# A fused two-block transformer with experts: the exponent's bias moved from VectorE to ScalarE, and the hand-kept order of the work planned anew

## The chip, the cores and the metric

One NeuronCore of a Trainium2 chip runs the whole program. The metric is the device time of one execution in microseconds. Three executions of the kernel before took 3205.08, 3207.56 and 3210.16 us; the median is 3207.56 us.

## The reference, cut to what matters

The input is 8 batches of 512 tokens of 256 numbers. Block L0 normalises, does self-attention and then cross-attention whose operands are rounded to 8 bits, and a gated feed-forward; block L1 does a causal self-attention, a cross-attention and a layer of 8 experts of which each token takes two. The change touches only the two quantised attentions of L0 (stage 0 and stage 1 of each batch):

```python
def _fq(x, delta, zp, n_bits):
    xi = _round_ste(x / delta) + zp
    xq = jnp.clip(xi, 0.0, 2.0 ** n_bits - 1.0)
    return (xq - zp) * delta

sim = jnp.einsum('bhid,bhjd->bhij', _fq(q, dq, 128.0, 8), _fq(k, dk, 128.0, 8)) * SCALE
attn = jax.nn.softmax(sim, axis=-1)
out = jnp.einsum('bhij,bhjd->bhid', _fq(attn, dw, 0.0, 8), _fq(v, dv, 128.0, 8))
```

There are 16 heads of 16 numbers. The softmax is made as exp(scale * s - scale * max), and the product scale * (-max) is the bias that this case is about.

## The kernel before, in words

The program has a transformer part (`transformer`, up to about 2640 us of the span) and behind it an experts part (`experts`). The transformer part is a list of about sixty kinds of steps for every batch B, stage s (0 and 1 quantised attention, 2 feed-forward, 3 and 4 exact attention, 5 and 6 last norm and routing) and number n. `program_steps` says what each step must wait for. `program_order` plays all steps through with `TIMES` (ns that a step takes of its engine, ns until its result is there), `HOPS` (ns from an engine's result to another engine) and `OWN_RESULT` (pairs of kinds where an engine waits for its own result). At every point it picks, among the steps that can start within `AHEAD` ns of the first one, the one with the highest rank: its distance to the end of the program plus an offset from the table `URGENT`. The resulting list `ORDER` is fixed when the program is built, and each engine issues its own kinds (table `ON`) in exactly this order. So an engine whose next step is not ready holds all its later steps back. Where the planner leaves TensorE a gap of `WARM_GAP` (400 ns) or more it puts in matmuls `W` whose result nobody reads (L1678).

A quantised attention stage has 32 units (`UNITS`) of two heads and 128 rows each; over 8 batches and 2 stages that makes 512 units. One unit u runs through this chain:

- `S` (TensorE, L1780): two matmuls put the scores 128x1024 into two PSUM banks. The banks come free when `E` of unit u-2 has read them.
- `M` (VectorE, L1493): `tensor_reduce` with max and negation gives `nmax`, 128x2.
- `nb` (VectorE, L1496): `tensor_scalar` multiplies `nmax` by the stage's scale, a column of `sc`, and gives `nbias`, 128x2. It waits for the engine's own `M`.
- `E` (ScalarE, L1645), twice, one per head: the exponential of 128x512 with `nbias` as bias and `sc` as scale, and the row sums. The first waits for `nb`.
- `R` and `RS` (VectorE, L1499 and L1502): the reciprocal of the row sums, and its product with the quantisation step, `rstep`.
- `Q` (GpSimd, L1263), twice: multiplies by `rstep` and rounds to integers in float16. It waits for `RS`.
- `T` (TensorE, L1788): 8 transposes. `ev` (VectorE, L1509): brings them to SBUF. `AV` (TensorE, L1800): the product with the values.

The exact attentions have their own chain: `A` (TensorE, L1811), `am` (VectorE, L1517, 1024 row maxima), `ms` (GpSimd), `MT` (TensorE), `mt` (ScalarE, L1653), `B` (TensorE, L1833), `E2` (ScalarE, L1664 and L1666), `AV2` (TensorE, L1850). The planner lays a quantised stage of one batch beside an exact stage or the feed-forward of another. ScalarE also empties the PSUM banks of the projections (L1560, L1590, L1606, L1613, L1614, L1620, L1627).

The two lines on VectorE that make the bias:

```python
if kind == "nb":
    after(dve, "M", B, s, n)
    nc.vector.tensor_scalar(nbias[:, n % 2, :], nmax[:, n % 2, :], sc[:, s:s + 1], None, ALU.mult).then_inc(SIG["nb"], 1)
```

Of the kernel before, what the change touches and what calls it, by code (L numbers as in the profile page):

```python
# [6 lines left out]
ALU = mybir.AluOpType  # L7
ACT = mybir.ActivationFunctionType
# [70 lines left out]
def place_taken(B):  # L79
# [29 lines left out]
ON = {"PE": "rT rL rP W S T AV A MT B AV2 xT cT k q v y g w z",  # L109
# [6 lines left out]
ROUTING_OPENS = ("A", 6, 3, 0)  # L116
AHEAD = 84
TIMES = {
# [6 lines left out]
    "own": (3600, 3600), "pkk": (1300, 5500), "pkq": (500, 4500), "psk": (500, 2700), "psq": (1300, 4500), "qi": (330, 417),  # L125
# [18 lines left out]
HOPS = {("PE", "DVE"): 38, ("PE", "ACT"): 38, ("DVE", "PE"): 70, ("ACT", "PE"): 80, ("POOL", "PE"): 56, ("DVE", "ACT"): 36, ("DVE", "POOL"): 83, ("ACT", "DVE"): 60, ("ACT", "POOL"): 80, ("POOL", "DVE"): 60, ("POOL", "ACT"): 90, ("PE", "POOL"): 40}  # L144
OWN_RESULT = {("M", "nb"), ("R", "RS"), ("ki", "ki"), ("qi", "qi"), ("vi", "vi"), ("spk", "spk"), ("spq", "spq"), ("xn", "gb"), ("xn", "bi"), ("rs", "xn"), ("dy", "st"), ("rl", "rl")}
URGENT = {
# [28 lines left out]
    ("pkk", 3): (18222,), ("pkk", 4): (-279907,), ("pkq", 3): (-102687,), ("pkq", 4): (-210459,), ("psk", 3): (70270,),  # L175
    ("psk", 4): (-17390,), ("psq", 3): (180111,), ("psq", 4): (157149,), ("q", 0): (-11596,), ("q", 1): (-58692,),
# [4 lines left out]
    ("spk", 3): (57020,), ("spk", 4): (-35279,), ("spq", 3): (58304,), ("spq", 4): (35133,), ("st", 0): (1581,),  # L181
# [6 lines left out]

# [607 lines left out]
def transformer(nc, scratch, by_row, x, ctx, w, mid, rows_in, kept, s_sc, s_zeroed, s_eb, s_block, s_expert):  # L796
# [41 lines left out]
    with ExitStack() as es:  # L838
# [24 lines left out]
        sc = sb("sc", [P, 4], F32)  # L863
# [7 lines left out]
        xn = sb("xn", [P, NT, D], F32)  # L871
        xT = sb("xT", [P, KT, N], F32)
# [425 lines left out]
        def _(dve):  # L1298
# [15 lines left out]
            for at, e in enumerate(ORDER):  # L1314
# [175 lines left out]
                if kind == "M":  # L1490
                    after(dve, "S", B, s, n)
                    a = BANKS[("S", B, s, n)][0]
                    nc.vector.tensor_reduce(nmax[:, n % 2, :], ps[:, a:a + 2, :], AX.X, ALU.max, negate=True).then_inc(SIG["M"], 1)  # L1493
                if kind == "nb":
                    after(dve, "M", B, s, n)
                    nc.vector.tensor_scalar(nbias[:, n % 2, :], nmax[:, n % 2, :], sc[:, s:s + 1], None, ALU.mult).then_inc(SIG["nb"], 1)  # L1496
                if kind == "R":
# [35 lines left out]
        def _(act):  # L1533
# [8 lines left out]
            for at, e in enumerate(ORDER):  # L1542
# [90 lines left out]
                if kind == "do":  # L1633
                    m = n
                    after(act, "AV", B, s, 2 * NT * m + 2 * NT - 1)
                    stage = before(Q_STAGES, B, s)
                    if stage and m == 0:
                        after(act, "y", *stage, NT - 1)
                    nc.scalar.activation(oTq[:, m, :], OUTQ, ACT.Identity, scale=sc[:, 2 + s:3 + s]).then_inc(SIG["do"], 1)
                if kind == "E":  # L1640
                    u, h = n // 2, n % 2
                    if h == 0:
                        after(act, "nb", B, s, u)
                    after_ordinal(act, "Q", NO[e] - 4)
                    nc.scalar.activation(probs[:, u % 2, h, :], ps[:, BANKS[("S", B, s, u)][h], :], ACT.Exp,  # L1645
                                         bias=nbias[:, u % 2, h:h + 1], scale=sc[:, s:s + 1],
                                         accum_out=rsum[:, u % 2, h:h + 1]).then_inc(SIG["E"], 1)
# [855 lines left out]
```

## Time and profile before

| | us |
|---|---|
| median of three executions | 3207.56 |
| the profiled execution, its own time | 3203.77 |
| span from its first to its last instruction | 3202.0 |
| TensorE busy | 2905.9 (91% of the span) |
| VectorE busy | 2257.2 (70%) |
| ScalarE busy | 1960.0 (61%) |
| GpSimd busy | 1497.5 (47%) |
| mean granted TensorE clock | 0.967 |

The span is 1.8 us shorter than the execution's own time. The busy times count an instruction from its start to its end, so two instructions of one engine that overlap are both counted within a group's sum. The share of the span is a mean over parts with different limits: the transformer part and the experts part are to be read apart, which the view by stretches allows.

### The profile page before, as it was taken

To read this page: it belongs to the slowest core of one execution; us is meant where nothing else is said; L and a number is where in the kernel's file an instruction comes from. 1 tells how busy PE (TensorE), PEld (TensorE's weight loads), DVE (VectorE), ACT (ScalarE), POOL (GpSimd) and SP (SyncE) were. 2 spreads that over 40 slices of the span, in tenths; PEclk is the share of its full clock that TensorE was granted. 3 is DMA by queue.
4 is the path that set the end of the run, shared out by engine and by line. 5 is a ranking of instruction groups with operands and counts; after the bars stand their busy time and mean duration, and the time that the engine had idled before them with its cause. 6 is when DMAs were issued, how large, how long until landed. Compare 5 with 4: busy or idle time off the path is not lost. (4 is left out here: it accounts for less than half of the span.)

```text
span 3202.0 us, 57992 instructions
## 1 busy us (share of the span) xinstructions
PE 2905.9 (91%) x19128; PEld 1688.7 (53%) x19128; DVE 2257.2 (70%) x5109; ACT 1960.0 (61%) x4167; POOL 1497.5 (47%) x2258
## 2 busy tenths in 40 slices
PE   5999989999999999899989999998889899999991
PEld 2445443544354445444543544354444459999991
DVE  3797797989798879978897989798856643111115
ACT  3676676765767676767676765766536354444442
POOL 4654482567266626644682667265714622111115
PEclk9999999999999999999999999998989899999996
DMA  4001321233132204220321222131143339999995
GB/s 112 24 11 47 99 64 53 66 74 90 34 91 72 69 22 106 56 76 27 113 73 43 69 71 77 34 100 53 53 156 91 117 115 329 327 326 326 325 329 162
DMA packets 264462, 358.82 MB, mean 112 GB/s; under 512 B 30558, under 2 KB 235486, under 8 KB 257808
## 3 DMA queue, kind: packets, MB, share of 16 engines
q1 hardware_dynamic: 254960, 336.97, 35.0%
q0 software_dynamic: 6480, 17.58, 1.5%
q8 instruction: 139, 2.28, 0.3%
q10 hardware_dynamic: 2768, 1.06, 0.1%
q14 instruction: 115, 0.94, 0.1%
HBM read 292.55 MB, written 64.86 MB: 112 GB/s over the span
## 5 line engine op out<-in xcount | busy, mean ns | idle before, releaser
L1645 ACT ACTIVATE quant<-ps,nbias,sc 128x512 f32<-128x512 f32 x1024 | 790.3, 778 | 266.9 <-DVE nbias L1496 202.3
L1263 POOL TENSOR_SCALAR quant<-quant,rstep 128x512 f16<-128x512 f32 x1024 | 714.2, 697 | 470.9 <-DVE rstep L1502 219.8
L1517 DVE TENSOR_REDUCE m<-ps 128x1 f32<-128x512 f32 (+3 forms) x1024 | 558.7, 582 | 219.4 <-PE ps L1811 139.0
L1493 DVE TENSOR_REDUCE nmax<-ps 128x2 f32<-128x1024 f32 x512 | 620.9, 1216 | 43.4 <-PE ps L1780 40.6
L2209 ACT ACTIVATE hT<-moe_ps,expert_b 128x128 f32<-128x128 f32 x568 | 207.6, 368 | 269.2 <-PE moe_ps L2123 231.0
L1811 PE MATMUL ps<-kst,qst 96*128 96x512 bf16 (+3 forms) x1024 | 322.8, 353 | 46.0 <-DVE m L1517 23.5
L1509 DVE TENSOR_SCALAR big<-ps 128x1024 bf16<-128x1024 f16 x512 | 347.8, 679 | 19.0 <-PE ps L1788 16.8
L1788 PE MATMUL ps<-id,quant 128*128 128x128 f16 x4096 | 321.5, 223 | 39.2 <-DVE big L1509 28.7
L1788 PEld LDWEIGHTS ps<-id,quant 128*128 128x128 f16 x4096 | 251.9, 99 | 194.4 <-issue 112.1
L1664 ACT ACTIVATE big<-ps 128x256 f32<-128x256 f32 (+1 forms) x608 | 251.1, 467 | 92.0 <-PE ps L1836 52.6
L2404 DVE COPY words<-plain_rows 128x3 uint32 x71 | 12.0, 169 | 417.8 <-PE moe_ps L2175 417.8
L1833 PE MATMUL ps<-qst,kst 108*128 108x512 bf16 (+3 forms) x1024 | 287.9, 345 | 16.3 <-ACT big L1664 7.5
L2065 POOL DMA_INDIRECT rows_out<-yb,words x71 | 69.2, 975 | 436.8 <-DVE yb L2411 436.8
L1758 PE MATMUL ps<-xT,wring 128*128 128x512 f32 x512 | 259.2, 615 | 1.4 <-ACT uT L1627 0.9
L1780 PE MATMUL ps<-quant 32*128 32x512 bf16 x1024 | 195.2, 393 | 57.1 <-ACT quant L1645 41.2
L1811 PEld LDWEIGHTS ps<-kst,qst 96*128 96x128 bf16 x1024 | 97.9, 98 | 261.4 <-DVE m L1517 183.2
L1678 PE MATMUL ps<-idb 128*128 128x512 bf16 x794 | 213.9, 384 | 23.5 <-DVE sc L1311 20.0
L1850 PE MATMUL ps<-big,v_f 128*32 128x512 f32 (+3 forms) x2048 | 229.5, 524 | 0.1
L1666 ACT ACTIVATE big<-ps 128x1024 f32<-128x1024 f32 x208 | 200.8, 1027 | 24.1 <-PE ps L1833 17.6
L1645 ACT ACTIVATION_READ_ACCUMULATOR quant<-ps,nbias,sc 128x1 f32 x1024 | 206.4, 202 | 0.0
L1735 PE MATMUL ps<-xT,wring 128*128 128x512 f32 x384 | 200.2, 623 | 5.5 <-ACT parts_sb L1614 2.0
L1653 ACT ACTIVATE qst<-ps 12x1024 bf16<-12x1024 bf16 x128 | 123.8, 1009 | 127.8 <-PE ps L1820 126.9
(292 smaller groups left out, 4953.8 us busy)
## 6 DMA issues: line engine op xcount, KB each, us to landing
e_w<-in_L_xattn_e_w_dram SPq DMA_DIRECT2D x70, 1024.0 KB, 7.5
quant<-in_L_xattn_e_w_dram SPq DMA_DIRECT2D x36, 1024.0 KB, 7.5
uT<-in_L_xattn_e_w_dram SPq DMA_DIRECT2D x36, 1024.0 KB, 6.9
wring<-in_L_xattn_ff_w_dram SPq DMA_DIRECT2D x96, 256.0 KB, 2.8
parts<-parts_sb SPq DMA_DIRECT2D x64, 384.0 KB, 2.9
qst<-parts SPq DMA_DIRECT2D x32, 768.0 KB, 5.7
kst<-parts SPq DMA_DIRECT2D x32, 384.0 KB, 4.7
plain_rows<-rows_in SPq DMA_DIRECT2D x71, 140.0 KB, 2.6
```

The costliest lines, as they stand in the source:

```text
L1263: nc.gpsimd.tensor_scalar(pq[:, u % 2, h, :], probs[:, u % 2, h, :], rstep[:, u % 2, h:h + 1], HALF_ROUND, ALU.mult, ALU.add).then_inc(SIG ...
L1493: nc.vector.tensor_reduce(nmax[:, n % 2, :], ps[:, a:a + 2, :], AX.X, ALU.max, negate=True).then_inc(SIG["M"], 1)
L1509: nc.vector.tensor_scalar(probs_t[:, g % 2, 2 * p:2 * p + 2, :, t * P:(t + 1) * P], PT, -HALF_ROUND, WMAX, ALU.add, ALU.min).then_inc(SIG[ ...
L1517: nc.vector.tensor_reduce(m32[:, g % 2, t, h:h + 1], bank(("A", B, s, n))[:, 0:width], AX.X, ALU.max, negate=True).then_inc(SIG["am"], 1)
L1645: nc.scalar.activation(probs[:, u % 2, h, :], ps[:, BANKS[("S", B, s, u)][h], :], ACT.Exp, bias=nbias[:, u % 2, h:h + 1], scale=sc[:, s:s ...
L1664: last = nc.scalar.activation(ex[:, half, h, j, i0:N], ps[:, from_, i0:N], ACT.Exp, scale=SCALE)
L1678: nc.tensor.matmul(ps[:, BANKS[e][0], :], idb[:, :], idb[:, :].unsqueeze(1).broadcast_to([P, NT, P]), start=True, stop=True)
L1758: last = nc.tensor.matmul(bank(e), wt[:, k, (f % 2) * P:(f % 2 + 1) * P], xT[:, k, :], start=(k == 0), stop=(k == KT - 1))
L1788: last = nc.tensor.transpose(PT[:, h, j, :], pq[:, n % 2, h, j * P:(j + 1) * P], id16[:, :])
L1811: last = nc.tensor.matmul(bank(e)[:, 0:width], qst[0:PAIR_ROWS, head, t * P:(t + 1) * P], kst[0:PAIR_ROWS, head, 0:width], start=True, sto ...
L1833: last = nc.tensor.matmul(dst[:, i0:N], kst[0:rows_, head, jt * P:(jt + 1) * P], qst[0:rows_, head, i0:N], start=True, stop=not causal(s))
L1850: last = nc.tensor.matmul(OUTX[SLOT * h:SLOT * (h + 1), i0:N], v_f32[:, jt, SLOT * head:SLOT * (head + 1)], ex[:, half, h, j, i0:N], start ...
```

## The change

The step `nb` moves from VectorE's list to ScalarE's. There it is an `activation` with the function Copy and the same column as scale, issued where the order has it, in front of the unit's exponentials; it waits for `M` on VectorE, and the first `E` waits for ScalarE's own result. The planner's tables follow: `nb` now counts 112 ns of its engine and 205 ns to its result instead of 136 and 228, the pair (nb, E) replaces (M, nb) among the own results, `AHEAD` goes from 84 to 96, and all offsets in `URGENT` are new (two lines of them are shown), so the order of all steps on all engines can differ.

```diff
-      "DVE": "own rl rm ri rp M nb R RS ev am n1 n3 st dy dz ki qi vi dV dw",
-      "ACT": "dr rx ry E do mt E2 dT dc dk dq dv dg ge",
+      "DVE": "own rl rm ri rp M R RS ev am n1 n3 st dy dz ki qi vi dV dw",
+      "ACT": "dr rx ry nb E do mt E2 dT dc dk dq dv dg ge",
...
-AHEAD = 84
+AHEAD = 96
...
-    "ms": (1075, 1092), "mt": (925, 1016), "n1": (905, 995), "n2": (576, 618), "n3": (614, 699), "nb": (136, 228),
+    "ms": (1075, 1092), "mt": (925, 1016), "n1": (905, 995), "n2": (576, 618), "n3": (614, 699), "nb": (112, 205),
...
-OWN_RESULT = {("M", "nb"), ("R", "RS"), ("ki", "ki"), ...
+OWN_RESULT = {("nb", "E"), ("R", "RS"), ("ki", "ki"), ...
 URGENT = {
-    ("A", 3): (133536, 113145, 237023, 266612), ("A", 4): (33371, 21778, -19736, 186228),
-    ("AV", 0): (-63268, -50853, -103134, -296192), ("AV", 1): (57219, -110289, -16902, -42897),
+    ("A", 3): (183146, 80339, 254450, 286905), ("A", 4): (17744, -11118, -2576, 173453),
+    ("AV", 0): (-50796, -81711, -88455, -404689), ("AV", 1): (187697, -119379, -89580, -52619),
...
-                if kind == "nb":
-                    after(dve, "M", B, s, n)
-                    nc.vector.tensor_scalar(nbias[:, n % 2, :], nmax[:, n % 2, :], sc[:, s:s + 1], None, ALU.mult).then_inc(SIG["nb"], 1)
...
+                if kind == "nb":
+                    after(act, "M", B, s, n)
+                    nc.scalar.activation(nbias[:, n % 2, :], nmax[:, n % 2, :], ACT.Copy, scale=sc[:, s:s + 1]).then_inc(SIG["nb"], 1)
```

## Rows read from the trace of the kernel before

**Rows 1.** The page: busy time of each engine over the whole span.

```profile
PE 2905.9 (91%) x19128; PEld 1688.7 (53%) x19128; DVE 2257.2 (70%) x5109; ACT 1960.0 (61%) x4167; POOL 1497.5 (47%) x2258
```

**Rows 2.** Stretches: start:end length, busy (count) of PE PEld DVE ACT POOL, clock, DMA.

```profile
2720.00:3120.00 400.00, 400.00 (x2765) 377.23 (x2763) 72.41 (x224) 177.23 (x497) 53.48 (x55) 1.00 0.98 327
240.00:2240.00 2000.00, 1867.22 (x12412) 950.06 (x12412) 1702.58 (x3631) 1397.55 (x2890) 1084.45 (x1677) 0.98 0.25 67
```

**Rows 3.** Stretches of L1678 alone, the matmuls that nobody reads.

```profile
240.00:2240.00 2000.00, 88.88 (x318) 28.07 (x317) 0.98 0.25 67
```

**Rows 4.** Six stretches of 80 us in which VectorE is fullest: one, and the sum.

```profile
400.00:480.00 80.00, 70.42 (x514) 36.50 (x515) 74.41 (x163) 60.29 (x145) 64.29 (x92) 0.98 0.25 64
...
sum 480.00, PE 430.04 PEld 222.29 DVE 453.48 ACT 332.10 POOL 342.00; mean PE 71.67 PEld 37.05 DVE 75.58 ACT 55.35 POOL 57.00
```

**Rows 5.** The same six stretches for L1678 alone.

```profile
sum 480.00, PE 89.62 PEld 29.03; mean PE 14.94 PEld 4.84
```

**Rows 6.** Three stretches of 80 us with both VectorE and TensorE full: the sum.

```profile
sum 240.00, PE 227.29 PEld 137.53 DVE 221.75 ACT 162.75 POOL 154.42; mean PE 75.76 PEld 45.84 DVE 73.92 ACT 54.25 POOL 51.47
```

**Rows 7.** L1496, the bias on VectorE: its group, its durations, who waited for it.

```profile
L1496 DVE TENSOR_SCALAR nbias<-nmax,sc 128x2 f32<-128x2 f32 x512 | 188.6, 372 | 2.0
L1496 DVE TENSOR_SCALAR nbias<-nmax,sc x512: 204/229/1181, 57.2 to 2288.3; 128x2 f32<-128x2 f32 x171
ACT quant L1645 <- DVE nbias L1496: 202.3, 225, 8.8
```

**Rows 8.** Timeline, a unit with no stall: start, duration, engine, line, operation, idle before.

```profile
167.92 1.21 DVE L1493 TENSOR_REDUCE nmax<-ps 128x2 f32<-128x1024 f32 x1
...
169.11 0.17 DVE L1499 RECIPROCAL rinv<-rsum 128x2 f32<-128x2 f32 x1
...
169.19 0.21 DVE L1496 TENSOR_SCALAR nbias<-nmax,sc 128x2 f32<-128x2 f32 x1
169.31 0.16 DVE L1502 TENSOR_TENSOR rstep<-rinv,inv_step 128x2 f32<-128x2 f32 x1
...
169.44 0.78 ACT L1645 ACTIVATE quant<-ps,nbias,sc 128x512 f32<-128x512 f32 x1 [0.36 <-DVE nbias L1496]
```

**Rows 9.** Timeline, two biases beside a GpSimd instruction.

```profile
408.78 1.16 POOL L1271 TENSOR_TENSOR kf<-kf,parts_sb 128x512 f32<-128x512 f32 x1 [0.21 <-ACT parts_sb L1614]
...
409.01 1.08 DVE L1496 TENSOR_SCALAR nbias<-nmax,sc 128x2 f32<-128x2 f32 x2
```

**Rows 10.** Timeline, R and RS with no bias between them, beside a GpSimd instruction.

```profile
723.66 0.17 DVE L1499 RECIPROCAL rinv<-rsum 128x2 f32<-128x2 f32 x1
723.68 1.16 POOL L1271 TENSOR_TENSOR kf<-kf,parts_sb 128x512 f32<-128x512 f32 x1
...
723.86 1.00 DVE L1502 TENSOR_TENSOR rstep<-rinv,inv_step 128x2 f32<-128x2 f32 x1
```

**Rows 11.** Durations of L1502 (least/median/most) and its group.

```profile
L1502 DVE TENSOR_TENSOR rstep<-rinv,inv_step x512: 95/154/1139, 59.4 to 2293.4; 128x2 f32<-128x2 f32 x171
L1502 DVE TENSOR_TENSOR rstep<-rinv,inv_step 128x2 f32<-128x2 f32 x512 | 104.1, 205 | 5.8
```

**Rows 12.** The same six stretches, and the same three, for L1496 alone.

```profile
sum 480.00, DVE 64.10; mean DVE 10.68
...
sum 240.00, DVE 25.23; mean DVE 8.41
```

**Rows 13.** Groups of ScalarE: a tiny activation; a drain without and with a column.

```profile
L1583 ACT ACTIVATE e<-dlt 128x4 f32<-128x4 f32 x7 | 1.5, 208 | 6.5 <-DVE dlt L1455 6.5
L1590 ACT ACTIVATE cT<-ps 128x512 f32<-128x512 f32 x32 | 19.3, 604 | 6.8 <-PE ps L1719 6.8
L1606 ACT ACTIVATE kf<-ps,inv_step 128x512 f32<-128x512 f32 x32 | 21.9, 686 | 22.9 <-PE ps L1735 22.2
```

**Rows 14.** Timeline of ScalarE: a drain and the table load that follows the GELU.

```profile
271.37 0.58 ACT L1590 ACTIVATE cT<-ps 128x512 f32<-128x512 f32 x1
271.96 1.28 ACT L1645 ACT_TABLE_LOAD   x1
```

More of the change, by code:

```diff
@@ L144 @@
 HOPS = {("PE", "DVE"): 38, ("PE", "ACT"): 38, ("DVE", "PE"): 70, ("ACT", "PE"): 80, ("POOL", "PE"): 56, ("DVE", "ACT"): 36, ("DVE", "POOL"): 83, ("ACT", "DVE"): 60, ("ACT", "POOL"): 80, ("POOL", "DVE"): 60, ("POOL", "ACT"): 90, ("PE", "POOL"): 40}
-OWN_RESULT = {("M", "nb"), ("R", "RS"), ("ki", "ki"), ("qi", "qi"), ("vi", "vi"), ("spk", "spk"), ("spq", "spq"), ("xn", "gb"), ("xn", "bi"), ("rs", "xn"), ("dy", "st"), ("rl", "rl")}
+OWN_RESULT = {("nb", "E"), ("R", "RS"), ("ki", "ki"), ("qi", "qi"), ("vi", "vi"), ("spk", "spk"), ("spq", "spq"), ("xn", "gb"), ("xn", "bi"), ("rs", "xn"), ("dy", "st"), ("rl", "rl")}
 URGENT = {
[28 rows of a table removed]
-    ("pkk", 3): (18222,), ("pkk", 4): (-279907,), ("pkq", 3): (-102687,), ("pkq", 4): (-210459,), ("psk", 3): (70270,),
-    ("psk", 4): (-17390,), ("psq", 3): (180111,), ("psq", 4): (157149,), ("q", 0): (-11596,), ("q", 1): (-58692,),
[4 rows of a table removed]
-    ("spk", 3): (57020,), ("spk", 4): (-35279,), ("spq", 3): (58304,), ("spq", 4): (35133,), ("st", 0): (1581,),
[6 rows of a table removed]
[28 rows of a table added]
+    ("pkk", 3): (27947,), ("pkk", 4): (-387624,), ("pkq", 3): (-139477,), ("pkq", 4): (-271711,), ("psk", 3): (-97826,),
+    ("psk", 4): (129271,), ("psq", 3): (251348,), ("psq", 4): (234996,), ("q", 0): (-60474,), ("q", 1): (-118565,),
[4 rows of a table added]
+    ("spk", 3): (42671,), ("spk", 4): (-51252,), ("spq", 3): (213338,), ("spq", 4): (207139,), ("st", 0): (-93484,),
[6 rows of a table added]
 PAIRED = UNITS - 8
```

72 rows, old and new, of the table URGENT are left out of this document.

## The prediction

> **What bounds the kernel now.** I read the whole first, then the stretches, then the operation that moves. The page has TensorE busy 91% of the span and VectorE 70% [rows 1], but the two halves differ. In the experts part TensorE is busy 400.0 of 400 us and the DMA engines 98% [rows 2]; the change touches nothing there, so it can only begin earlier. In the transformer part from 240 to 2240 us TensorE is busy 1867.2 of 2000 us and VectorE 1702.6, ScalarE 1397.6, GpSimd 1084.5 [rows 2]. Of TensorE's time 88.9 us is matmuls that nobody reads [rows 3]; with the 132.8 us in which it is not busy, it has 221.7 us of slack in 2000. VectorE is second, but not evenly. In six stretches of 80 us (from 160, 400, 720, 1280, 1600 and 1920 us) it is busy 453.5 of 480 us, or 94%; TensorE is busy 430.0, of which 89.6 is filler [rows 4, 5], so VectorE and its chain set the pace there. In three more (from 880, 1200 and 2080 us) both are full: VectorE 221.8 of 240, TensorE 227.3 [rows 6]. Everywhere else TensorE's own work or a chain of waits sets the pace.
>
> **What the bias costs on VectorE.** 512 instructions took 188.6 us, mean 372 ns, though the median is 229 ns and the longest 1181 [rows 7]. A typical one is short: R starts at 169.11, the bias at 169.19, RS at 169.31 [rows 8]. The excess over the median is 188.6 - 512 x 0.229 = 71 us, and it has a cause that can be seen: two biases that start at 409.01 take 1.08 us together, and GpSimd's two-input instruction runs from 408.78 to 409.94 [rows 9]. So the bias waits until GpSimd's instruction is over. ScalarE waited for the bias 225 times, 202.3 us in all [rows 7].
>
> **What is removed.** (a) In 247 of the 512 units the bias stands between R and RS, as in [rows 8]. There RS starts 0.20 us after R; with no bias between them it starts 0.20 us after R as well (723.66 and 723.86, [rows 10]), because RS waits for R's result. In these units the plain bias costs nothing, and only its stall can go: 247/512 of 71, or 34 us. RS can inherit it: with no bias in front, the RS at 723.86 took 1.00 us beside a GpSimd instruction that ended at 724.84 [rows 10], and RS has a median of 154 ns and a mean of 205 [rows 11]. Between all and nothing I take half, 17 us. (b) In the other 265 the bias takes a place of its own: at least the 0.12 us from its start to the next start [rows 8], at most its 0.23; I take 0.15, so 40 us, and the stall of 37 us goes. Sum: 17 + 40 + 37 = 94 us of VectorE. The ends are 265 x 0.12 = 32 us (every stall turns up in another instruction) and 188.6 us (all of it).
>
> The Trainium skill (SBUF — State Buffer, Who interferes with whom) says that a VectorE instruction with two SBUF inputs also contends with a GpSimd instruction that reads SBUF, and that ScalarE waits for nobody. By that rule the stall of (a) would all go over to RS and the 94 would be 77. The row at 723.86 agrees; the mean of RS leaves open how often.
>
> **What of it lies on the path.** The six stretches hold 64.1 us of the bias's 188.6 (0.34), the three full ones 25.2 (0.13) [rows 12]. In the six a saving counts, in the three I count half, since TensorE's own work is next in line there. Share: 0.34 + 0.13/2 = 0.405. So 94 x 0.405 = 38 us off, with ends of 13 and 76. Elsewhere I cost the removal at nothing: TensorE's work covers it.
>
> **What is added.** The activation of 128x2 with a column as scale is not in the trace. The nearest row, an activation of 128x4 without a column, took 208 ns; a column adds 686 - 604 = 82 ns [rows 13]. So 0.29 us, with 0.21 and 0.37 (two columns' worth) as ends. With about 0.04 us behind it for the own result (E started 0.04 after the bias ended, [rows 8]) ScalarE is held for 0.33 us a unit, 169 us in all. The planner reckons with 112 and 205 ns, less than this. A table load took 1.28 us, and a drain right after the GELU ran without one [rows 14]; in front of the exponential it comes in any case, so I add none for Copy.
>
> (c) Where ScalarE waited for the bias (225 units), the way from M's end to E was 169.13 to 169.44, 0.31 us [rows 8]; it will be 0.04 + 0.29 + 0.04 = 0.37. That is 225 x 0.06 = 14 us, on the path 14 x 0.405 = 5 us. (d) In the other 287 the bias was ready when ScalarE came, and 287 x 0.33 = 95 us are new work in its line, 38 us at the same share. Cover: ScalarE is busy 332.1 of 480 us in the six stretches [rows 4]. If it has a gap behind each such unit this costs 0, if none 38; it sits idle 31% of the time, and banks of scores are double, so I take a quarter: 10 us. If that cover goes, what comes late is what stands behind it on ScalarE: E2 and the drains, and TensorE behind those. (e) The bias on ScalarE waits for M, and everything behind it too; but E stood in the same line and waited for the same chain, so no new kind of wait arises if the bias stands directly before E. No DMA is moved on any queue.
>
> **Sum.** -38 + 5 + 10 = -23 us against the profiled execution's 3203.8 us gives 3180.8. The median of the executions shown is 3.8 us above that one, so 3184 us. With the ends alone: -76 + 5 + 0 gives 3136, -13 + 5 + 38 gives 3238. The new order is a term that I can't read from rows; it was made with a price for the bias that is 0.08 us too low and with no stalls at all, so I put it at zero and let it widen the range. A measurement of this kernel can tell about 0.2%, 6 us, from no change.
>
> **The rivals.**
> - *Twice the gain.* With VectorE relieved the new order fills a third of TensorE's slack of 221.7 us: -74, about 3134 us. For it: the filler sits just where VectorE is full [rows 4, 5]. Against: where both are full [rows 6] there is nothing to fill. Chance 0.10.
> - *Nothing.* RS inherits the stalls and the price of (d) lands in full: -77 x 0.405 + 5 + 26, about 3207 us. The TensorE-bound stretches speak for it. Chance 0.13.
> - *Slower: ScalarE becomes the blocker.* The place is ScalarE's line in the six stretches. Only the low saving arrives (13 us), and (c) and (d) land in full, 5 + 38: +30, about 3238 us. It decides from the point where ScalarE has no gap left behind a unit, which shows as TensorE waiting for E2, E and the drains. The six stretches hold 0.34 of the 512 units, 174; 0.33 us each adds 57 to 332 of 480 us, 81% busy: near, not there. Chance 0.20, the lesser outcomes on that side included.
> - *The change doesn't do what it says.* Excluded: the instruction is gone from VectorE.
>
> **How the numbers follow.** The forecast, 3160 to 3201 us, has 0.57. So faster by over 0.2% is 0.57 + 0.10 = 0.67, within 0.2% 0.13, slower 0.20. The range goes from 3142 (most of the low end and part of the first rival) to 3222 (half way to the last rival); about a tenth is left out on either side.
>
> **What the next profile would show.** L1496's 188.6 us are gone from VectorE and an ACTIVATE of about 0.29 us x512 stands on ScalarE, about 150 us. VectorE's total falls by more than 150 us; RS's mean rises above 205 ns (inherited stall) but by less than 70. The filler in 240 to 2240 us falls below 88.9. ScalarE's wait now names M, some 250 us or less. I am wrong if RS takes over all of the stall, if TensorE's waits for ScalarE's E, E2 and drains grow by over 40 us, or if the experts part doesn't start earlier although VectorE has been relieved.

## The result and the profile after

The changed kernel takes 3212.97 us (median of 12 executions, 3209.91 to 3218.10); run beside it, the kernel before takes 3203.84 us (12 executions). The ratio is 1.0029, with a 95% interval of 1.0020 to 1.0038: slower by 9 us. The forecast was 3184 us, 23 us faster; the time lies within the range given, but on the other side of no change. The clock is not the reason: the profiled execution of the changed kernel was granted 0.975 in the mean, that of the kernel before 0.967.

The page of the changed kernel, busy time of each engine over a span of 3208.9 us (answers to [rows 1]):

```profile
PE 2922.2 (91%) x19253; PEld 1686.5 (53%) x19253; DVE 2151.0 (67%) x4597; ACT 2069.9 (65%) x4679; POOL 1491.5 (46%) x2258
```

VectorE has 106 us less, ScalarE 110 us more. The operations behind that, as groups (busy us, mean ns, idle before and its releaser); they answer to [rows 7], [rows 11] and [rows 13]. The last two lines are the reciprocal and the filler in the kernel before:

```profile
L1639 ACT ACTIVATE nbias<-nmax,sc 128x2 f32<-128x2 f32 x512 | 150.8, 297 | 115.1 <-DVE nmax L1493 112.5
L1499 DVE TENSOR_TENSOR rstep<-rinv,inv_step 128x2 f32<-128x2 f32 x512 | 133.8, 262 | 8.3
L1496 DVE RECIPROCAL rinv<-rsum 128x2 f32<-128x2 f32 x512 | 80.2, 157 | 103.5 <-ACT quant L1645 101.1
L1678 PE MATMUL ps<-idb 128*128 128x512 bf16 x919 | 255.1, 388 | 28.9 <-DVE sc L1311 19.8 <-DVE X L1335 5.0 <-ACT xT L1557 3.1
...
L1499 DVE RECIPROCAL rinv<-rsum 128x2 f32<-128x2 f32 x512 | 79.8, 156 | 54.4 <-ACT quant L1645 52.5
L1678 PE MATMUL ps<-idb 128*128 128x512 bf16 x794 | 213.9, 384 | 23.5 <-DVE sc L1311 20.0
```

The bias costs ScalarE 297 ns apiece. RS rises from a mean of 205 to 262 ns: 29.7 us more. And VectorE, before its reciprocal, now waits 101 us for ScalarE's exponential; in the kernel before that was 52.5 us. The matmuls that nobody reads grow from 794 to 919; their number is fixed by the planner when the program is built, so it tells of the new plan and not of how the run went.

Stretches, columns as in [rows 2]: the long one, then the sum of the six and the sum of the three of [rows 4] and [rows 6]; last, the six for L1678 alone, as in [rows 5]:

```profile
240.00:2240.00 2000.00, 1869.89 (x12436) 947.80 (x12434) 1599.65 (x3216) 1479.81 (x3287) 1081.09 (x1677) 0.99 0.25 68
...
sum 480.00, PE 430.31 PEld 221.62 DVE 426.36 ACT 377.34 POOL 342.50; mean PE 71.72 PEld 36.94 DVE 71.06 ACT 62.89 POOL 57.08
...
sum 240.00, PE 229.18 PEld 136.54 DVE 204.46 ACT 177.98 POOL 164.37; mean PE 76.39 PEld 45.51 DVE 68.15 ACT 59.33 POOL 54.79
...
sum 480.00, PE 93.99 PEld 28.62; mean PE 15.67 PEld 4.77
```

In the six, VectorE falls from 453.5 to 426.4 us of 480 and ScalarE rises from 332.1 to 377.3, but TensorE does no more than before, and more of it is filler (94.0 for 89.6 us). A stretch at the clock holds slightly different work in the two kernels, so these sums show how full the engines are, not what was saved.

A closer look at the changed kernel, in a stretch where TensorE has only a quantised stage and filler, beside which [rows 8] stands (start, duration, engine, line, operation, idle before). First ScalarE, then VectorE; the last line is the first exponential of the unit after that of [rows 8], in the kernel before:

```profile
169.96 0.30 ACT L1639 ACTIVATE nbias<-nmax,sc 128x2 f32<-128x2 f32 x1
170.29 0.78 ACT L1645 ACTIVATE quant<-ps,nbias,sc 128x512 f32<-128x512 f32 x1
...
171.06 0.77 ACT L1645 ACTIVATE quant<-ps,nbias,sc 128x512 f32<-128x512 f32 x1
...
171.86 0.29 ACT L1639 ACTIVATE nbias<-nmax,sc 128x2 f32<-128x2 f32 x1
172.19 0.78 ACT L1645 ACTIVATE quant<-ps,nbias,sc 128x512 f32<-128x512 f32 x1
...
175.29 0.78 ACT L1645 ACTIVATE quant<-ps,nbias,sc 128x512 f32<-128x512 f32 x1 [1.30 <-POOL quant L1263]
...
170.31 0.38 DVE L1499 TENSOR_TENSOR rstep<-rinv,inv_step 128x2 f32<-128x2 f32 x1
170.61 1.21 DVE L1493 TENSOR_REDUCE nmax<-ps 128x2 f32<-128x1024 f32 x1
171.75 0.68 DVE L1506 TENSOR_SCALAR big<-ps 128x1024 bf16<-128x1024 f16 x1
172.40 1.22 DVE L1493 TENSOR_REDUCE nmax<-ps 128x2 f32<-128x1024 f32 x1
...
171.50 0.78 ACT L1645 ACTIVATE quant<-ps,nbias,sc 128x512 f32<-128x512 f32 x1 [0.43 <-DVE nbias L1496]
```

From bias to exponential it is 0.33 us (169.96 to 170.29, 171.86 to 172.19), as reckoned: the exponential has to wait for ScalarE's own result. In the kernel before ScalarE had a gap of 0.36 us at this place [rows 8]; now the exponentials and the bias fill the whole 1.90 us of a unit. VectorE has no gap here either: RS, the maximum and `ev` follow on each other. And the unit isn't slower: it takes 1.90 us where the kernel before takes 2.06 (169.44 to 171.50). A little later ScalarE sits idle for 1.30 us, until GpSimd has freed a buffer. So this stretch shows where ScalarE's gap went, and no loss; what the loss is made of only the experiments tell.

### The profile page after: what moved, and what is told of

Same layout as the page of the kernel before. It is cut to its first block and busy times, and to the rows that moved or that the text cites. A ratio compares the mean times of both kernels' runs of the same rounds, so it can differ in the third digit from the quotient of the medians.

```text
span 3208.9 us, 58225 instructions
## 1 busy us (share of the span) xinstructions
PE 2922.2 (91%) x19253; PEld 1686.5 (53%) x19253; DVE 2151.0 (67%) x4597; ACT 2069.9 (65%) x4679; POOL 1491.5 (46%) x2258
## 5 line engine op out<-in xcount | busy, mean ns | idle before, releaser
L1678 PE MATMUL ps<-idb 128*128 128x512 bf16 x919 | 255.1, 388 | 28.9 <-DVE sc L1311 19.8
L1758 PE MATMUL ps<-xT,wring 128*128 128x512 f32 x512 | 258.5, 608 | 2.6 <-ACT uT L1624 0.8
L1780 PE MATMUL ps<-quant 32*128 32x512 bf16 x1024 | 191.1, 389 | 47.7 <-ACT quant L1645 28.9
L1639 ACT ACTIVATE nbias<-nmax,sc 128x2 f32<-128x2 f32 x512 | 150.8, 297 | 115.1 <-DVE nmax L1493 112.5
```

The costliest lines, as they stand in the source:

```text
L1678: nc.tensor.matmul(ps[:, BANKS[e][0], :], idb[:, :], idb[:, :].unsqueeze(1).broadcast_to([P, NT, P]), start=True, stop=True)
L1758: last = nc.tensor.matmul(bank(e), wt[:, k, (f % 2) * P:(f % 2 + 1) * P], xT[:, k, :], start=(k == 0), stop=(k == KT - 1))
```

## The experiments

Each time is a ratio to the kernel before, run beside it on the same chip, with its 95% interval. Where a text gives microseconds for a difference of ratios, it is the difference times 3204; by their intervals, such differences are good to 4 to 9 us.

### The move alone, in the old order

The planner's tables are those of before, so all engines keep their order; the bias is issued on ScalarE directly in front of the unit's first exponential.

```diff
-                if kind == "nb":        # VectorE
-                    after(dve, "M", B, s, n)
-                    nc.vector.tensor_scalar(nbias...)
...
                 if kind == "E":         # ScalarE
                     if h == 0:
-                        after(act, "nb", B, s, u)
+                        after(act, "M", B, s, u)
+                        nc.scalar.activation(nbias[:, u % 2, :], nmax[:, u % 2, :], ACT.Copy, scale=sc[:, s:s + 1]).then_inc(SIG["nb"], 1)
+                        after(act, "nb", B, s, u)
```

> The order of all steps is that of the kernel before, and only the bias moves: it is issued on ScalarE directly in front of the unit's first exponential. Theory 1 (the move is good or neutral and the new order lost the time): within 0.3% of before or faster, 3180 to 3207 us. Theory 2 (ScalarE's 0.30 us in the chain costs more than VectorE gets back): slower than before by 0.2 to 1%, 3212 to 3235 us, and TensorE's waits for ScalarE grow. In both RS's mean goes up from 205 ns, to about 260.

Measured: 1.0020 (1.0007 to 1.0034). The move by itself costs about 6 us. That is at the lower edge of what theory 2 gave, and inside theory 1's "within 0.3%", so this run alone doesn't decide between them; the next ones do. RS has a mean of 268 ns.

### No bias product at all

The exponential takes a bias of zero, so this kernel leaves out the subtraction of the row maximum; M itself and its wait stay.

```diff
-                    nc.vector.tensor_scalar(nbias[:, n % 2, :], nmax[:, n % 2, :], sc[:, s:s + 1], None, ALU.mult)
...
-                        after(act, "nb", B, s, u)
+                        after(act, "M", B, s, u)
```

> The order of before, with the bias product left out on every engine: the exponential takes a bias of zero, but still waits for the row maximum. This is the most that can be had from taking the bias off both engines. Theory 1 and my prediction's on-path share (0.4 of VectorE's relief): 20 to 40 us faster, 3165 to 3185 us. Theory 3 (the path runs through TensorE and the fixed order, VectorE's relief is hardly on it): less than 10 us faster, 3194 to 3204 us.

Measured: 0.9913 (0.9892 to 0.9935), 28 us faster. So VectorE's relief is on the path, and the move to ScalarE gives back all of it and more: from 0.9913 to 1.0020 is 34 us for ScalarE's part, the way from maximum to exponential included, which this kernel has not and the kernel before has. RS's mean goes to 297 ns: even with nothing in front of it but R, part of the stall stays on VectorE.

```profile
L1500 DVE TENSOR_TENSOR rstep<-rinv,inv_step 128x2 f32<-128x2 f32 x512 | 151.9, 297 | 14.1
```

### The product on VectorE, read by nobody

As the last one, with a bias of zero (the maximum isn't subtracted), but VectorE still makes the product in its old place.

```diff
-                        after(act, "nb", B, s, u)
+                        after(act, "M", B, s, u)
...
-                                         bias=nbias[:, u % 2, h:h + 1], scale=sc[:, s:s + 1],
+                                         bias=sc[:, 4:5], scale=sc[:, s:s + 1],
```

> The order of before, the product stays on VectorE in its place, but nobody reads it: the exponential takes a bias of zero and waits for the row maximum alone. Against the run without any product this adds VectorE's part alone; against before it takes the product's latency out of the chain alone. Theory 4 (the gain of leaving the product out came mostly from VectorE's relief): within 0.3% of before, 0 to 10 us faster. Theory 5 (it came mostly from the shorter way from maximum to exponential): 15 to 27 us faster than before.

Measured: 0.9984 (0.9972 to 0.9996). The way from maximum to exponential through VectorE's product is worth 5 us; VectorE's own relief, 0.9984 to 0.9913, is worth 23 us. For it VectorE's busy time falls by 77 us between the two kernels (2251.9 and 2174.9 on their pages). Theory 4 holds.

### A product on ScalarE, read by nobody, behind or in front of the exponentials

Both have a bias of zero (the maximum isn't subtracted) and no product on VectorE. The first puts the activation behind the second exponential, the second directly in front of the first one, which doesn't wait for its result.

```diff
+                    if h == 1:          # the first kernel
...
+                        nc.scalar.activation(nbias[:, u % 2, :], sc[:, 0:2], ACT.Copy, scale=sc[:, s:s + 1]).then_inc(SIG["nb"], 1)
```

```diff
                     if h == 0:          # the second kernel
...
                         after(act, "M", B, s, u)
+                        nc.scalar.activation(nbias[:, u % 2, :], nmax[:, u % 2, :], ACT.Copy, scale=sc[:, s:s + 1]).then_inc(SIG["nb"], 1)
```

The lines left out make the activation wait for its own forerunner of two units before.

> The order of before, no product on VectorE, bias of zero, and an activation of the same size on ScalarE behind the unit's second exponential, that waits for nothing and is read by nobody. It adds ScalarE's occupancy (about 0.2 us a unit, 102 us in all) to the run without any product, and no latency. Theory 2a (ScalarE's occupancy is the price): 15 us or more slower than the run without any product. Theory 2b (the price is the wait for the own result in the chain, not the occupancy): less than 8 us slower than it.

Measured: 0.9934 (0.9918 to 0.9950), 7 us above the run without any product. This is theory 2b: the occupancy is cheap, 7 us for 157.6 us that the activations are busy.

> As the run with a product on ScalarE that nobody reads, in the order of before and with a bias of zero, but it now stands between the wait for the row maximum and the first exponential, which doesn't wait for its result. If standing in front of the exponential is the price, it is 10 to 20 us slower than the run that has it behind the second one (0.9934 of before), at 0.997 to 1.000 of before, and the wait for the own result makes up the rest to the real move (1.002). If the own result's wait is nearly all of the price, it stays below 0.995 of before.

Measured: 0.9942 (0.9922 to 0.9962), 9 us above the run without any product. The place in front of the exponential isn't the price either. What separates this kernel from the move alone (1.0020) is only that the exponential reads the bias and so waits for it: 25 us. Its timeline, to be laid beside that of the changed kernel:

```profile
170.32 0.28 ACT L1643 ACTIVATE nbias<-nmax,sc 128x2 f32<-128x2 f32 x1
170.50 0.77 ACT L1645 ACTIVATE quant<-ps,sc 128x512 f32<-128x512 f32 x1
...
172.09 0.30 ACT L1643 ACTIVATE nbias<-nmax,sc 128x2 f32<-128x2 f32 x1
172.30 0.76 ACT L1645 ACTIVATE quant<-ps,sc 128x512 f32<-128x512 f32 x1
```

Here the exponential starts 0.18 to 0.21 us behind the activation, since the two overlap; with the real dependency it is 0.33 us. The difference of some 0.14 us, in which ScalarE starts nothing else, comes in nearly all of the 512 units: 72 us at most, of which 25 end up in the time.

### The product on ScalarE at the bias's old place in the order

```diff
-                if kind == "nb":        # VectorE
+                if kind == "nb":        # ScalarE, at the same place of ORDER
```

> The order of before, the product on ScalarE, but at the place in the order that it had on VectorE, so that in 147 of 512 units other work of ScalarE stands between it and the exponential and hides its result's way. Theory 2b: 3 to 10 us faster than the run with the product directly in front of the exponential. Theory 2a: within 3 us of it. If the product now waits for its maximum too early and blocks drains, it is slower than it.

Measured: 1.0009 (0.9999 to 1.0018), 4 us less than the move directly in front. Where other work of ScalarE stands between the two, it can hide the way of the own result. The intervals of the two overlap, so this agrees with theory 2b but doesn't show it by itself.

### The product on GpSimd

```diff
+                if kind == "nb":        # GpSimd, at the same place of ORDER
+                    after(pool, "M", B, s, n)
+                    nc.gpsimd.tensor_scalar(nbias[:, n % 2, :], nmax[:, n % 2, :], sc[:, s:s + 1], 0.0, ALU.mult, ALU.add)
```

> The order of before, the product on GpSimd at the same place of the order. GpSimd is the least busy engine (54% in 240 to 2240 us) and a tiny instruction took it 0.20 us. If the blocking of ScalarE is what costs, this is faster than the move to ScalarE, 5 to 15 us faster than before; if GpSimd's own line (the quantisation of the unit before) holds the product back, it is 5 to 30 us slower than before.

Measured: 1.0139 (1.0121 to 1.0156). Slower by 44 us: the emptiest engine isn't the cheapest place.

```profile
L1645 ACT ACTIVATE quant<-ps,nbias,sc 128x512 f32<-128x512 f32 x1024 | 791.4, 779 | 314.2 <-POOL nbias L1267 245.6 <-POOL quant L1263 66.2
L1267 POOL TENSOR_SCALAR nbias<-nmax,sc 128x2 f32<-128x2 f32 x512 | 137.5, 269 | 136.7 <-DVE nmax L1496 109.4 <-PE ps L1788 0.2
```

The product waits 109 us for its maximum at the head of GpSimd's line, with the quantisations behind it, and ScalarE waits 246 us for it.

### The plans crossed

Three kernels in which the planner or its order meets a split that it wasn't made for, and one with an honest price.

```diff
-AHEAD = 84                              # kernel before, bias on VectorE,
+AHEAD = 96                              # with the new offsets in URGENT
```

> The bias stays on VectorE, and the planner runs with the new offsets and the new look-ahead. Theory 1 (the new plan is worse in itself): slower than before by 5 to 20 us. Theory 2 (the move costs, the plan is not to blame): 3195 to 3206 us. The plan isn't made for this engine split, so a loss here alone doesn't decide.

Measured: 1.0328 (1.0306 to 1.0350).

```diff
                 if kind == "M":         # the changed kernel's order, VectorE
+                    after(dve, "M", B, s, n)
+                    nc.vector.tensor_scalar(nbias...)
```

> The order of the changed kernel, with the bias back on VectorE directly behind each row maximum. Theory 1 (the order lost the time, the move itself gained): slower than the changed kernel, 3220 us or more. Theory 2 (the move lost it): 3200 us or less.

Measured: 1.0267 (1.0244 to 1.0291).

```diff
-AHEAD = 96                              # changed kernel, bias on ScalarE,
+AHEAD = 84                              # with the old offsets in URGENT
```

> The changed kernel with the offsets and the look-ahead of the kernel before: the planner runs again with the bias on ScalarE, but with offsets found for the other split. With before's order kept, the move cost 0.2%; with the new plan 0.3%. If planning anew with fitting offsets is what keeps the changed kernel near before, this one is 1 to 4% slower than before, as the two crossed plans were. If offsets matter little, it is within 0.5% of before.

Measured: 1.0205 (1.0191 to 1.0219).

```diff
-    "nb": (112, 205),                   # changed kernel
+    "nb": (205, 295),
```

> The changed kernel, with the planner's price of the bias set to what its trace shows, 205 ns of ScalarE and 295 ns to the result, in place of 112 and 205; offsets and look-ahead stay. If the price that is too low cost the time: 5 to 15 us faster than the changed kernel, level with before or below. If the offsets only fit the plan they were found with: 20 to 100 us slower, as the other runs that planned with offsets made for another engine split.

Measured: 1.0172 (1.0155 to 1.0190). The price alone, corrected, makes the plan 46 us worse than the changed kernel: these offsets fit the prices with which they were found and none of the others tried. So none of these four tells whether the new plan is good; they tell that these offsets can't be carried over to another price or split, and that runs planned anew can't be laid beside each other to price an edit. Whether offsets found with the honest price would help wasn't tried. The changed plan (1.0029) and the old order with the same move (1.0020) lie within each other's intervals, so against this move planning anew gained nothing that can be measured. Against the better place in the old order (1.0009, 0.9999 to 1.0018) the changed plan even loses 6 us, and these two intervals don't meet. In e_stay_new_order the bias stands at a place that the old plan never gave it, so its loss isn't the new order's alone.

### The product on VectorE in the form that also gives an accumulator

```diff
-                    nc.vector.tensor_scalar(nbias[:, n % 2, :], nmax[:, n % 2, :], sc[:, s:s + 1], None, ALU.mult)
+                    after_ordinal(dve, "nb", NO[e] - 1)
+                    nc.vector.tensor_scalar(nbias[:, n % 2, :], nmax[:, n % 2, :], sc[:, s:s + 1], 0.0, ALU.mult, ALU.add,
+                                            accum_out=sc[:, 4:5])
```

The bias products all write the same dead column `sc[:, 4:5]`, so each waits for the one before it. In the next two kernels RS does the same with a column of its own.

> The kernel before, its order too, the product still on VectorE, but in the form that also gives an accumulator. The Trainium skill (SBUF - State Buffer, Who interferes with whom) states that this form doesn't take the port pair that VectorE shares with GpSimd. If the rule holds: the product's mean falls from 372 to about 230 ns, with some 65 ns behind it for reading the accumulator, and the stall partly goes over to RS; the time is 0 to 10 us below before. If not: the mean stays at 370 ns and the time rises by 5 to 15 us.

Measured: 0.9933 (0.9917 to 0.9950), 21 us faster than before, with nothing moved. The reading of the accumulator, for whose 65 ns I had no row, takes 82 ns. Durations (least/median/most) and the group of RS:

```profile
L1497 DVE TENSOR_SCALAR_CACHE_REDUCE nbias<-nmax,sc x512: 165/214/218, 57.6 to 2273.6; 128x2 f32<-128x2 f32 x171
L1497 DVE DVE_READ_ACCUMULATOR nbias<-nmax,sc x512: 75/82/86, 57.7 to 2273.7; 128x1 f32 x171
...
L1504 DVE TENSOR_TENSOR rstep<-rinv,inv_step 128x2 f32<-128x2 f32 x512 | 142.5, 279 | 5.8
```

The longest of 512 is 218 ns, where it was 1181 [rows 7]: the stall on the bias is gone altogether. RS takes over 38 of its 71 us.

### Both small products in that form

```diff
-                    nc.vector.tensor_tensor(rstep[:, n % 2, :], rinv[:, n % 2, :], inv_step[...].broadcast_to([P, 2]), ALU.mult)
+                    nc.vector.tensor_scalar(rstep[:, n % 2, :], rinv[:, n % 2, :], inv_step[:, 4 * s + 3:4 * s + 4], 0.0, ALU.mult, ALU.add,
+                                            accum_out=sc[:, 5:6])
```

> The kernel before with its order, and both small products of VectorE, the bias and the step, in the form that also gives an accumulator. With the bias alone in this form it was at 0.9933 of before and the step's mean rose from 205 to 279 ns. If what is left is the stall that went over to the step, its mean falls to about 210 ns and the time to 0.985 to 0.991 of before. If the 0.08 us of reading the accumulator eats it, the time stays at 0.992 to 0.995.

Measured: 0.9874 (0.9857 to 0.9891), 3165.54 us beside 3205.26 us: 40 us faster than before. It computes everything that the reference does, and it beats both kernels.

```profile
PE 2896.0 (92%) x19128; PEld 1687.5 (53%) x19128; DVE 2197.3 (69%) x6133; ACT 1955.7 (62%) x4167; POOL 1495.3 (47%) x2258
...
L1505 DVE TENSOR_SCALAR_CACHE_REDUCE rstep<-rinv,inv_step 128x2 f32<-128x2 f32 x512 | 107.9, 211 | 8.0 <-issue 0.8 <-DVE rinv L1501 0.3
L1497 DVE TENSOR_SCALAR_CACHE_REDUCE nbias<-nmax,sc 128x2 f32<-128x2 f32 x512 | 107.1, 209 | 4.6 <-issue 0.3
```

VectorE's busy time falls by only 60 us, less than by the move (84 with the order held, 2257.2 to 2173.1; 106 in the changed kernel), yet the time falls by 40. No product of VectorE is left that GpSimd holds up, and ScalarE has no product to wait for.

### The same form for the step in the changed kernel

> The changed kernel and its order, with only the step's product in the form that gives an accumulator, so that it can't inherit the bias's stall (its mean was 262 ns). If VectorE is still on the path in the changed kernel, the time is 0.2 to 0.6% below the changed kernel's, 0.997 to 1.001 of before. If ScalarE's line has taken over, it is within 0.1% of the changed kernel, 1.002 to 1.004 of before.

Measured: 1.0013 (1.0003 to 1.0023), beside 1.0029 of the changed kernel. RS falls from 262 to 209 ns, and the end of its stall is worth 0.16% here, 5 us; with the bias on VectorE the same edit was worth 0.9933 to 0.9874, 19 us. The result lies between the two cases expected. It points to ScalarE's line having taken VectorE's place on much of the path, not on all of it.

### Bias and maximum in one instruction

```diff
-                    nc.vector.tensor_reduce(nmax[:, n % 2, :], ps[:, a:a + 2, :], AX.X, ALU.max, negate=True)
+                    for h in range(2):
+                        nc.vector.tensor_scalar(ps[:, a + h, :], ps[:, a + h, :], sc[:, 4 + s:5 + s], None, ALU.mult, ALU.min,
+                                                accum_out=nbias[:, n % 2, h:h + 1]).then_inc(SIG["nb"], 1)
...
-                                         bias=nbias[:, u % 2, h:h + 1], scale=sc[:, s:s + 1],
+                                         bias=nbias[:, u % 2, h:h + 1], scale=-1.0,
```

> The order of before, but no product on any engine as a step of its own: VectorE multiplies the scores of one head by the negative scale in place in PSUM and takes their minimum in the same instruction, which is the bias; the exponential then has scale -1 as an immediate. Two instructions of 512 elements (about 0.65 us each with the reading of the accumulator) replace the 1.22 us maximum and the product; the first exponential can start after the first half; each exponential loses one column operand (82 ns by the drains with and without one). Expected: VectorE's busy time 40 to 80 us lower, ScalarE's about 80 lower, the time 25 to 50 us below before. If reading the accumulator takes much more than 65 ns, or PSUM in place is slow, it is level with before or slower.

Measured: 0.9993 (0.9981 to 1.0005), no difference.

```profile
PE 2904.1 (91%) x19128; PEld 1689.0 (53%) x19128; DVE 2254.0 (70%) x6134; ACT 1891.2 (59%) x4167; POOL 1500.4 (47%) x2258
...
L1495 DVE TENSOR_SCALAR_CACHE_REDUCE ps<-ps,sc 128x512 f32<-128x512 f32 x1024 | 726.5, 752 | 42.5 <-PE ps L1779 41.6
L1495 DVE DVE_READ_ACCUMULATOR ps<-ps,sc 128x1 f32 x1024 | 143.1, 140 | 0.0
```

The instruction takes 752 ns where I reckoned 650 with the reading. VectorE ends where it was (2254.0 for 2257.2 us) and ScalarE has 69 us less. The time doesn't move. That fits a ScalarE whose relief is worth nothing while VectorE is as full as before; but the chain changed too, and RS rose from 205 to 269 ns here, so the run doesn't show it alone.

## Why the prediction was wrong, point by point

Two terms failed, by about the same amount, and it took both to turn the sign: what of VectorE's relief lies on the path (38 us forecast, 23 measured), and the wait for ScalarE's own result (5 us forecast, 20 measured). With either one as forecast and the other as measured, the sum would still have been 8 or 9 us on the fast side. By the intervals, each of these measured terms is good to 8 or 9 us.

- **What bounds the kernel.** Right: VectorE's chain sets the pace of the quantised stages. Taking the product off it gives 28 us with the shorter way, and bringing it and RS into the accumulator form gives 40.
- **(a) and (b), what is removed.** 94 us off VectorE were forecast. The page of the changed kernel has 106, but with the order held it is 84 for the move and 77 for the product alone (2251.9 to 2174.9). RS took over 29.7 us in the changed kernel and 33 us in the move alone (268 for 205 ns, 512 times), nearly all of the 34 us of (a), where I took half; with no product anywhere it took over 48 (297 ns), so some of the stall of (b) goes to it as well. The Trainium skill's rule (SBUF — State Buffer, Who interferes with whom) put all of (a) there, and the runs side with the rule: its sum was 77. It also gave the form that ended the stall.
- **The share of the path, the first step that failed.** 38 us were forecast for VectorE's relief; with the way from maximum to exponential left out on both sides, it measures 23 (0.9984 to 0.9913). That is within its ends of 13 and 76, but too high by 15 us. A third of this is the size of the relief (94 for 77 us), the rest the share: 23 of 77 is 0.30, where I had 0.405 by counting all that falls into the six full stretches. Which of the stretches gave less isn't known.
- **(d), the occupancy.** Right in size: 10 us forecast, 7 to 9 measured (0.9913 to 0.9934 and to 0.9942). But the argument, "it sits idle 31% of the time, and banks of scores are double, so I take a quarter", was applied to the whole 0.33 us, as if the wait for the own result could be covered like the activation itself.
- **(c) and (e), the wait for the own result, the second step that failed.** The price of one instruction was right, 0.29 us and 0.33 to the exponential. (c) put the longer way at 5 us, for 225 units; (e) says "no new kind of wait arises". One does: 0.14 us of the 0.33 are there only because the exponential needs ScalarE's own result, in every unit, and this is worth 25 us (0.9942 to 1.0020). The dependence on VectorE's product, which it replaces, was worth 5. So 20 us are new. All together: -23 + 9 + 20 is the +6 of the move alone. Why the wait costs so much more than the occupancy isn't shown by a run of its own; what the traces have is that VectorE waited 112 us for the exponential before its reciprocal in the move alone, 82 when the exponential didn't need the product, and 52.5 in the kernel before.
- **The new order.** Put at zero. It measures 3 us of loss against the move directly in front, not distinguishable from none, and 6 us against the better place. Near enough, but by luck: the offsets hold the level only for the prices with which they were found, and I knew nothing of that.
- **The rivals.** The one that ended slower named the engine. Its mechanism was the occupancy in full, 38 us, and that measured 9; its sign, TensorE waiting more for ScalarE, is faint with the order held and absent in the changed kernel (TensorE waits 41.2 us for the exponentials before it makes scores in the kernel before, 57.0 in the move alone, 28.9 in the changed kernel). Its point of decision, 81% busy in the six stretches, was not reached either: they show 377.3 of 480, 79%. The rival "nothing" has a slip in its sum: the price of (d) in full is 38 us and not 26, which makes it +12, about 3219 us. That the time lies in the range at all comes from the width that the slower rival gave it.
- **What I said the profile would show.** The bias on ScalarE (150.8 us), ScalarE's wait for M (112.5 us) and RS at 262 ns, within the band given, came true. VectorE's total fell by 106 us, not by more than 150: I added up durations of instructions that overlap. The filler from 240 to 2240 us rose to 117.3 us instead of falling, but it was no sign of anything: its number is planned, 794 in every kernel with the order of before, the one that is 40 us faster included. Of the signs of being wrong one came: the experts part starts later and not earlier, at 2619.3 us instead of 2613.2. RS didn't take over all of the stall, and TensorE's waits for ScalarE didn't grow by 40 us.

## What to carry to other kernels

When a small operation moves between engines, price two things apart: the time that it keeps its new engine busy, which was cheap here (9 us), and the wait of the next instruction for its own engine's result, which was not (25 us), although it is only 0.14 us apiece. The engine's idle share speaks for the first at most. Before moving a small instruction whose mean is far above its median, ask what makes it stall: ending the stall of two such products gave 40 us here, while the move passed 33 of the bias's 71 us of stall on to the next instruction. In a kernel with an order planned by tables, hold the order fixed when an edit is to be measured.

## What the runs showed of the hardware that I had not expected

- A 128x2 `tensor_scalar` in the accumulator form has no stall at all beside GpSimd (most 218 ns of 512), against 1181 ns in the plain form; the reading behind it takes 82 ns. The plain product of two SBUF inputs does stall (RS up to 1125 ns in the same run).
- The accumulator form with 128x512 in PSUM, in place, takes 752 ns and its reading 140 ns, so two of them cost more than one maximum over 1024 elements (1216 ns).
- Two activations that don't depend on each other start 0.18 to 0.21 us apart when the first is 128x2, though it lasts 0.28 to 0.30 us; with the dependency it is 0.33 us.
